# Shared feed-forward passes of two groups each, started two groups later, in a single-core attention and mixture-of-experts kernel

## The reference, cut to what matters

```
x = x + attention(layernorm(x), ctx, ctx, itok)
xt = layernorm(x)
logits = xt @ gate_w ; top 2 of 8 experts, at most 320 tokens each and choice
sh = gelu(xt @ sw1 + sb1) @ sw2 + sb2
sh = sh + gelu(xt @ swd) @ swu          # rank 32
out = x + sum over 2 choices of weight * expert(xt) + 0.2 * sh
```

## Time and profile before

| what | us |
|---|---|
| runs of the kernel before | 1335.53 to 1337.95, median 1337.92 |
| the profiled execution, its own time | 1338.04 |
| its span, first to last instruction | 1336.2 |
| busy in the span: PE | 1293.7 |
| DVE | 841.5 |
| ACT | 708.5 |
| POOL | 253.1 |

### The profile page before, as it was taken

How to read it: one execution, slowest core, us unless ns; L and a number is a source line. 1 busy time by engine, 2 the same in 40 slices (tenths; PEclk the granted TensorE clock), 3 DMA queues, 4 the chain that set the end, 5 groups by cost and what they waited for, 6 DMA issues and landing times.

```text
span 1336.2 us, 26800 instructions
## 1 busy us (share of the span) xinstructions
PE 1293.7 (97%) x10963; PEld 943.0 (71%) x11024; DVE 841.5 (63%) x1420; ACT 708.5 (53%) x1056; POOL 253.1 (19%) x219
## 2 busy tenths in 40 slices
PE   6788999999999999999999999999999999999997
PEld 2152736465554646384888889999999988888895
DVE  7777779797888887763742835638266383562730
ACT  5867676758676776662533524535244353442521
POOL 4740010000000051514200302203022030120112
PEclk7899999999999999999999999999999999999999
DMA  9614141423284332416736757677586775867313
GB/s 283 217 33 126 48 119 41 119 56 99 68 79 98 80 80 88 120 33 127 216 106 142 197 140 213 143 157 197 135 210 140 138 203 139 196 153 137 96 25 40
DMA packets 195627, 168.21 MB, mean 126 GB/s; under 512 B 117945, under 2 KB 138569, under 8 KB 195506
## 3 DMA queue, kind: packets, MB, share of 16 engines
q1 hardware_dynamic: 183218, 141.30, 40.7%
q0 software_dynamic: 12288, 25.21, 11.1%
HBM read 109.47 MB, written 34.15 MB: 107 GB/s over the span
## 4 chain that ended last, share of the span: by engine, by line
PE 88%; ACT 4%; issue 2%; DVE 2%; DMA 2%; SPq 1%; POOLq 0%; POOL 0%; another core or an unknown queue 0%; ACTq 0%; DVEq 0%
PE banks L1920 25%; PE banks L1950 24%; PE banks L1854 12%; PE banks L1836 10%; PE banks L1776 5%; PE banks L1756 4%; PE banks L1724 3%; ACT QS L1137 1%; DMA split_parts<-hidden 1%; PE banks L1810 1%; PE banks L1785 1%; ACT hf L1196 1%; ACT hidden L1150 1%; PE banks L1961 1%; PE banks L1822 1%
## 5 line engine op out<-in xcount | busy, mean ns | idle before, releaser
L1950 PE MATMUL banks<-hidden,w2h 128*128 128x0 bf16 x2048 | 306.1, 269 | 0.0
L1150 ACT ACTIVATE hidden<-banks,scales 128x512 f32<-128x512 f32 x256 | 170.4, 688 | 86.4 <-PE banks L1756 55.3
L1950 PEld LDWEIGHTS banks<-hidden,w2h 128*128 128x128 bf16 x2048 | 198.6, 98 | 20.5
L1378 DVE TENSOR_REDUCE rowmax<-banks 128x1 f32<-128x512 f32 x256 | 172.8, 686 | 33.0 <-PE banks L1724 31.6
L1950 PE MATMUL banks<-hidden,w2l 128*128 128x0 bf16 x1024 | 192.3, 269 | 0.0
L1529 DVE TENSOR_TENSOR w1l<-stage,w1h 128x2048 bf16<-128x2048 f32 x32 | 73.2, 2292 | 187.7 <-ACT w1h L1227 187.7
L1854 PE MATMUL banks<-w2h,hidden 128*128 128x512 bf16 x498 | 179.1, 379 | 0.8 <-issue 0.5
L1244 ACT ACTIVATE hf<-banks,b1cols 128x640 f32<-128x640 f32 x128 | 101.4, 793 | 122.4 <-PE banks L1920 108.8
L1255 ACT ACTIVATE yT<-banks 128x640 uint16<-128x640 uint16 x56 | 36.4, 702 | 215.2 <-PE banks L1950 215.2
L1920 PE MATMUL banks<-eth,w1h 128*128 128x0 bf16 x1024 | 133.0, 273 | 0.0
L1920 PE MATMUL banks<-etl,w1h 128*128 128x0 bf16 x1024 | 132.9, 273 | 0.0
(11 more groups left out here) (199 smaller groups left out, 1966.4 us busy)
## 6 DMA issues: line engine op xcount, KB each, us to landing
stage<-in_L_ffn_w SPq DMA_DIRECT2D x64, 1024.0 KB
split_parts<-hidden SPq DMA_DIRECT2D x16, 512.0 KB, 4.9
QS<-split_parts SPq DMA_DIRECT2D x48, 128.0 KB, 2.7
KS<-split_parts SPq DMA_DIRECT2D x48, 128.0 KB, 3.2
xin<-in_x SPq DMA_DIRECT2D x16, 256.0 KB, 3.8
cin<-in_ctx SPq DMA_DIRECT2D x16, 256.0 KB, 3.9
out_rows<-xin SPq DMA_DIRECT2D x16, 256.0 KB, 2.0
normed_rows<-x2r SPq DMA_DIRECT2D x16, 256.0 KB, 3.4
```

What stands on the lines that cost most here:

```text
L1150: ac.activation(prob[n % NPH], bank(score_bank[unit]), ACT.Exp, scale=scales[:, g // 2:g // 2 + 1]).then_inc(s_exp, 1)
L1378: dv.reduce_max(rowmax[g % 2][:, i:i + 1], bank(score_bank[unit]), X_AXIS).then_inc(s_max, 1)
L1950: issued = mm(bank(b0 + j)[:, skips[j]:CAP].shape_from_register(used_cols(e, j)), w[:, fb, rows], of_choice(a[:, fb, :], j, skips[j]).shap ...
```

## The change

`FIRST` now cuts the groups into 8 passes of two groups. The exponentials of groups 0, 1, 2 and 3 come in a row (`ahead_of_passes`, called four times), with the scores of the next group between them, up to four of the next but one at the end; no pass runs beside them. Window w then does `down` of pass w-2 and `rank` and `up` of pass w-1. The eight weight quarters are loaded and split two per group over the first three groups, one in the fourth, and the last one in the first pass (SP waits for POOL before that load, since it shares `late_stage` with the one before). Group 2 leaves `SUMMED`. The rank features are made by quarters: 48 matmuls of 64 columns with 32 weight columns each, four of them on four strips of PE's columns, instead of 12 of 256 columns with 96 weight columns (three copies); ACT's gelu of them takes four pieces, DVE writes the three copies. From pass 1 on they are in bank 3, which `ones` then waits for.

```diff
-FIRST = [0, *range(1, GROUPS, PASS // P), GROUPS]
+FIRST = [*range(0, GROUPS + 1, PASS // P)]
-SUMMED = [2, *range(4, GROUPS)]
+SUMMED = [*range(4, GROUPS)]
-AHEAD = 10
+AHEAD = 4
     def exponentials_and_down(w):
-        downs = [shared_down(w - 1, c) for c in range(len(groups_of(w - 1)))]
+        downs = [shared_down(w - 2, c) for c in range(len(groups_of(w - 2)))]
...
-        for n, _ in enumerate(shared_up(w)):
+        for n, _ in enumerate(shared_up(w - 1)):
...
+            if w == 1:
+                if n == 5:
+                    add("w_load", 7)
+                elif n == 9:
+                    add("w_split", 7)
+                elif n > 9:
+                    low_pieces()
...
+    def ahead_of_passes(g, score, side):
+
+        rows = max_rows(g + 1)
+        ahead = scores((g + 2) * UNITS, (g + 3) * UNITS)
         for i in range(UNITS):
+            add("exp", g, i)
             next(score, None)
+            if i >= UNITS - AHEAD and g < 2:
+                next(ahead)
+            if i == UNITS - AHEAD and g < 3:
+                add("parts", g + 1)
+            elif i > UNITS - AHEAD and g < 3:
                 next(rows)
+                if i > UNITS - AHEAD + 1:
+                    next(rows, None)
+            side(i)
+            if i < 4 and g:
+                half_step(g - 1, i + 10)
             if i > 5:
+                half_step(g, i - 6)
...
+    def split_and_lows(i, n, first, then):
+        if i == first:
+            add("w_split", n)
+        if i == then:
+            add("w_split", n + 1)
+        if first < i < first + 5 or i > then:
+            low_pieces()
...
+    def beside_first(i):
+
+        split_and_lows(i, 0, 5, 11)
+        if i == 0:
+            add("norm", 2)
+        if i == 1:
+            units(2, "x_hi", "x_lo", "c_lo", "bounce")
+            for n in range(2, 4):
+                add("w_load", n)
...
+        if i == 13:
+            add("b2_parts")
...
+    def beside_second(i):
+
+        split_and_lows(i, 2, 5, 11)
+        if i == 0:
+            add("norm", 3)
+        if i == 1:
+            units(3, "x_hi", "x_lo", "c_lo", "bounce")
+            for n in range(4, 7):
+                add("w_load", n)
+        if i == 4:
+            for _ in average(0):
+                pass
+            units(0, "stats2", "aggr2", "rstd2")
...
+        if i == 7:
+            add("norm2", 0)
+            add("load", 4)
+            add("c_load", 4)
...
+        if i == 13:
+            units(4, "stats", "aggr", "rstd")
...
+    for g, side in enumerate((beside_first, beside_second, beside_third, beside_fourth)):
+        score = ahead_of_passes(g, score, side)
...
-    for w in range(WINDOWS):
+    for w in range(1, WINDOWS):
...
                     w = P * len(groups_of(p))
...
-                    b = shared_bank(unit)
+                    b = 3 if rank_in_sums(p) else shared_bank(unit)
...
+                    q = w // RANK_TILES
                     for weights, data in ((wdh, xth[p % 2]), (wdh, xtl[p % 2]), (wdl, xth[p % 2])):
                         for kb in range(KB):
                             n += 1
-                            issued = mm(bank(b)[0:WIDE, 0:w], weights[:, kb, :], data[:, kb, 0:w], start=n == 1, stop=n == 3 * KB)
+                            for c in range(RANK_TILES):
+                                issued = mm(bank(b)[c * RANK:(c + 1) * RANK, 0:q], weights[:, kb, :],
+                                            data[:, kb, c * q:(c + 1) * q], start=n == 1, stop=n == 3 * KB)
```

More of the change, by code:

```diff
@@ L254, in next_scores @@
         def next_scores():
-            for _ in scores((a + 2) * UNITS + (EARLY if w else AHEAD), (a + 3) * UNITS):
+            for _ in scores((a + 2) * UNITS + EARLY, (a + 3) * UNITS):
                 yield
@@ L276, in up_pass @@
                     add("ones", b)
-            if w == 0 and n in (2, 3):
-                add("turn_v", a + n)
             if n == 3 and a + 4 < GROUPS:
@@ L341, in first_scores @@
         units(1, "stats", "aggr", "rstd")
-        score = scores(0, UNITS)
-        for i, _ in enumerate(score):
+        for i, _ in enumerate(scores(0, UNITS)):
             if i == 1:
@@ L358, in first_scores @@
                 add("scales")
-            if 2 < i < 7:
-                low_pieces()
+            if i == 13:
+                units(2, "stats", "aggr", "rstd")
         add("parts", 0)
-    def first_exponentials():
-        score = scores(UNITS, 2 * UNITS)
-        for _ in max_rows(0):
-            pass
-        for _ in range(4):
-            next(score)
-        rows = max_rows(1)
+    def ahead_of_passes(g, score, side):
+        rows = max_rows(g + 1)
+        ahead = scores((g + 2) * UNITS, (g + 3) * UNITS)
@@ new lines, in ahead_of_passes @@
+        if g < 3:
+            for _ in rows:
+                pass
+        return ahead
+    def split_and_lows(i, n, first, then):
[14 more added lines that the diff above has]
+        if i == 7:
+            add("fills", 1)
+        if i == 9:
+            units(3, "stats", "aggr", "rstd")
+        if i == 13:
+            add("b2_parts")
@@ new lines, in beside_third @@
+    def beside_third(i):
+        split_and_lows(i, 4, 6, 11)
+        if i == 0:
+            add("norm", 4)
+        if i == 1:
+            units(4, "x_hi", "x_lo", "c_lo", "bounce")
+        if i == 4:
+            for _ in average(1):
+                pass
+            units(1, "stats2", "aggr2", "rstd2")
+        if i == 6:
+            add("turn_v", 3)
+        if i == 7:
+            add("norm2", 1)
+            add("load", 5)
+            add("c_load", 5)
+        if i == 9:
+            add("turn", 1)
+            add("split_v", 4)
+        if i == 11:
+            units(1, "gate", "xt_lo", "logit")
+        if i == 13:
+            units(5, "stats", "aggr", "rstd")
+        if i == 15:
+            add("wd", E)
@@ new lines, in work_order, with beside_fourth @@
+    early_scores = scores(4 * UNITS, 4 * UNITS + EARLY)
+    def beside_fourth(i):
+        if i == 12:
+            add("w_split", 6)
+        if i > 12:
+            low_pieces()
+        if i == 0:
+            add("norm", 5)
+        if i == 1:
+            units(5, "x_hi", "x_lo", "c_lo", "bounce")
+        if i == 4:
+            for _ in average(2):
+                pass
+            units(2, "stats2", "aggr2", "rstd2")
+        if i == 5:
+            add("join_v", 4)
+            add("split_v", 5)
+        if i == 7:
+            add("norm2", 2)
+        if i >= UNITS - EARLY:
+            next(early_scores)
+        if i == 9:
+            add("turn", 2)
+        if i == 11:
+            units(2, "gate", "xt_lo", "logit")
+        if i in (2, 14):
+            for _ in rows2(i // 14):
+                pass
@@ L439, in work_order @@
+    first_scores()
+    for _ in max_rows(0):
+        pass
+    score = scores(UNITS, 2 * UNITS)
+    for _ in range(AHEAD):
+        next(score)
+    for g, side in enumerate((beside_first, beside_second, beside_third, beside_fourth)):
+        score = ahead_of_passes(g, score, side)
+        if g > 1:
+            score = iter(())
+    low_pieces(1)
     first_part, early, placed, routing = [], [], [], []
-    for w in range(WINDOWS):
+    for w in range(1, WINDOWS):
         if 2 * w == PARTS[1]:
@@ L731, in build @@
                         score_before[unit] = ("score", g, i - 2)
[L732 removed]
+                elif unit[0] == "score" and i >= UNITS - LATE and g % 2 and g > 3:
                     score_bank[unit] = 2 + i % 2
@@ L758, in build @@
                 first_place = len(shared_unit)
-            if (unit[0] in ("rank", "up") or (unit[0] == "down" and unit[3] == 0)
+            if unit[0] == "rank" and rank_in_sums(unit[1]):
+                shared_bank_of[unit] = 3
+            elif (unit[0] in ("rank", "up") or (unit[0] == "down" and unit[3] == 0)
                     or (unit[0] == "turn" and unit[1] and unit[1] % 2 == 0)):
```

182 lines of the change are left out of this document (63 added, 119 removed).

## The result

The changed kernel takes 1349.49 us, median of 4 runs (1347.71 to 1356.07), against 1337.93 of the kernel before (1335.53 to 1338.09): a ratio of 1.0105, 95% interval 1.0084 to 1.0126. It is 1.05% slower. Here that quotient is 1.0086, so small differences between ratios whose intervals overlap are not to be relied on. The prediction said 1331.3 us, and its range ended at 1341. The profiled execution took 1350.19 us with a span of 1348.4. In the experiments, one run each of e3, e4 and e6 (1925 to 7602 us) and one of the kernel before beside e14 (1373.46 us) lay far off and are in no ratio.

A forecast was written before the change was run, and what follows sets the result against it. PE's work bounds the kernel from the second pass on; ahead of that no engine is full. Front 118 + rest 1211.0 + last split 0.5 = 1329.5 us span, with 1.84 outside 1331.3, against 1338.04; range 1324 to 1341.

The forecast's parts named there:

- Part 1, the tail: After the windows: a full pass, `up` of 256 columns and four downs take 88.1 us, 17.4 more (17.4 to 20.8).
- rival E: Savings don't come: rank features no cheaper (+3.7 us), the last pass's odd 3.4 us again; 1338 us, chance 0.09.
- Part 2, the rank features: Six windows between front and tail: 429.25 us less 0.6 each for cheaper rank features, 3.7 in all.
- a microsecond a window, 6 in all: Six windows: cost if ACT's gelu in pieces and DVE's third copy were no longer covered beside PE.
- Part 3, the front: Ahead of the first `up`: four groups' exponentials in a row and the handover, ending at 118 us.
- X: Start of the first `up`: forecast 118 us, from 113 to 122; the change breaks even at 125.2.
- Group 1: 22.6: Front, group 1's exponentials: 22.4 us before, less a transfer wait and splits, plus copies, maxima and a late load.
- Group 2: 21.7: Front, group 2's exponentials: 19.1 us plus 1.05 for ACT's copy of ctx plus 1.5 for more maxima.
- the late load of group 4: Front, group 1: load of group 4's x queued behind weight quarters; nothing to 5 us, 2 taken.
- C: Front: DVE becomes the bound, late maxima hold scores and exponentials; X = 126 to 129, 1339 to 1342 us, chance 0.14.
- D: Front: the clock falls in groups 2 and 3, +3.5 us each; X = 125, 1338 us, chance 0.08.
- the signs that the prediction gave for being wrong in the front: PE waiting for maxima near bias parts or group 4's `stats` (xin releasing DVE); clock under 0.8 between 70 and 115.

The follow-up runs named there:

- e3: Changed kernel with the rank features as before (12 matmuls of 256 columns), still in bank 3 from pass 1 on; ratio to before 1.0083.
- e4: Kernel before with the rank features by quarters alone, its passes, order and banks kept; ratio to before 1.0019.
- e6: Changed kernel, copy ahead of weight split, weight quarters 4 to 6 behind group 4's load, average spread over steps, second norm a step later; ratio 1.0107.
- e14: e13 with the transposes of the values (`turn_v`) of groups 2 and 3 two steps later; ratio to before 1.0022.
- e13: Changed kernel, rank features of before, copy ahead of weight split, weight quarters 4 to 6 behind group 4's load, averages in two or three parts; ratio 1.0051.

## Why the prediction was wrong

**Part 1, the tail**: right. `up` of the full pass 21.24 us (21.0) without an idle piece, so rival E's 3.4 us did not return; the downs 42.23 (42.1). The last window's pass took 26.09 for 25.0. Of that the quarters make 0.6; the other 0.5 stands in e3 too (25.49), where it fits that this stretch now holds rank features for 256 tokens and before for 128.

**Part 2, the rank features**: "0.6 saved, six times", and "that costs nothing" for ACT's gelu in four pieces and DVE's third copy. The duration was not the trouble (0.7 taken, 0.49 measured, within its bounds). What failed is that their cover was judged by DVE's busy share over the whole window (349.97 of 429.25). At the head of the pass DVE works without a gap, so PE's saving is worth nothing there and DVE's 0.3 us are on the path: 72.1 us a window where 71.1 was forecast. That is the price the prediction itself named for the case that the cover is gone, "a microsecond a window, 6 in all", and did not put into its sum. Shown is the edit's 0.2% on the wrong side by e4's time and by the 3 us behind the first `up`. This is rival E's first half and more.

**Part 3, the front**: X = 118, measured 129.4. The first exponential (26.28 for 26.7), group 0 (21.67 for 22.7) and group 3 with the handover (22.21 for 22.0) came within 1.1 us of what was worked out; the failed terms are "Group 1: 22.6" and "Group 2: 21.7", measured 29.18 and 30.06. They were built from differences of engine time, and the 118 from 1.64 us of work per us; both hold only as long as the order of the queues lets the engines work. Three places were in the code and not in the sum: the copy behind a split (5.0 us of waits on DVE, 1.3 when moved), the average in one piece (4.14 us of standstill on ACT), `turn_v` ahead of its bank (2.1 us of PE's waits). The fourth, the late load of group 4, was in the sum with 2 us and its wait measured 2.1, but it was partly covered by the copy's: 4.8 once that was gone. Removing them one after another, with the rank features of before, took the ratio from 1.0105 to 1.0022, that is 0.83 of the 1.05 percent points, 0.2 of them by the rank features. What each place is worth by itself is not told apart, except that e14 is clear of e13.

The miss is not explained in full. The kernel was to be 0.5% faster, and e14 is 0.2% slower than before. Its median of 1339.98 us, less the 1.84 outside the span and the 1216.1 behind the first `up`, puts the first `up` at some 122 (an estimate) for 118; these 4 us are open. In e14 PE still waits 6.9 us for `MS` and 6.6 us for maxima (22 to 128 us). Of the signs that the prediction gave for being wrong in the front two came, PE waiting for maxima and an xin transfer as DVE's releaser.

**The rivals.** C named the mechanism, one late maximum holding the score and the exponentials behind it, and put it at X = 126 to 129, with a chance of 0.14. Its condition, that DVE becomes the bound, did not come true: DVE was busy 75.41 of 103.12 us. It was late, not full. D had groups 2 and 3 near a clock of 0.6; they had 0.83 and 0.92, the whole front 0.86, and raising it gave nothing that the times show.

## What to carry to other kernels

When a change packs stages together, don't only sum engine time; walk each queue and ask at each instruction that can wait what stands behind it and who wants that. Put what nobody is waiting for (a weight split, a low part, transposes for the next group) behind what others wait for, and cut long pieces on one engine so that a short urgent operation can come between. A hidden operation is hidden only if its engine has gaps at that place; the share over a window doesn't say so.

## What was not expected of the hardware

48 column-tiled matmuls of 64 columns, four quarters of PE at a time, took 0.49 us from the first to the score behind them (201.30 to 201.79), 10 ns each; with 160 columns it was 19.6. The Trainium skill (TensorE: Matmul & The Clock Gate, "Wait — 56ns, not 53.3ns?") has starts no closer than some 25 ns; the measurement decides.

Gelu of 32 x 64 in four pieces took ACT 0.90 us, of 96 x 256 in one piece 0.38 (timelines of after and e3 at the pass's head). A piece with a quarter of the columns took 0.22 us, well over a quarter of 0.38, so cutting such a short operation into pieces costs.
